# A decoder on one Trainium2 core: the C products of two of sixteen states in GpSimd's queue

## The reference, cut to what matters

```
xz = x @ Win;  xi, z = split(xz)
xi = silu(causal_dwconv(xi));  dt_in, B, C = split(xi @ Wx)      # 8, 16 and 16 columns
dt = softplus(dt_in @ Wdt + bdt);  A = -exp(Alog)
h[t, d, s] = exp(dt[t, d] * A[d, s]) * h[t-1, d, s] + dt[t, d] * xi[t, d] * B[t, s]
y[t, d]    = sum over s of h[t, d, s] * C[t, s]  +  xi[t, d] * D[d]
out = (y * silu(z)) @ Wout
```

## Time and profile before

| | us |
|---|---|
| median of three runs | 5442.49 |
| the profiled execution, its own time | 5428.83 |
| span of its trace | 5427.1 |
| the state-space stage in it | about 0 to 2475 |
| VectorE busy in 75 to 2475 | 2319 of 2400 |
| GpSimd busy in 75 to 2475 | 1974 of 2400 |
| TensorE's granted clock there, share of full speed | 0.91 |

### The profile page before, as it was taken

The page is one execution under the profiler, slowest core; times in us unless marked ns, Lnnn a source line. Parts: engine busy times, 40 slices in busy tenths (PEclk is TensorE's granted clock), DMA queues, the critical chain, the costliest instruction groups (busy, mean ns, idle before and its releaser), DMA issues. The chain is left out here.

```text
span 5427.1 us, 104523 instructions
## 1 busy us (share of the span) xinstructions
PE 4056.8 (75%) x29692; PEld 2331.6 (43%) x29692; DVE 4319.6 (80%) x8453; ACT 2781.0 (51%) x6469; POOL 3163.7 (58%) x3426
## 2 busy tenths in 40 slices
PE   5878778887787778874888678883747788688843
PEld 2333333333333333332666456652735666466611
DVE  5999999999999999994888767763356777666678
ACT  4555555555555555552777534434654445344434
POOL 5888888878888888874777533326452222333302
PEclk8998999889989989986999889995877888799955
DMA  2111111111110111102655366544125555465511
GB/s 84 67 49 54 69 68 68 42 62 69 68 69 33 69 68 68 69 37 46 105 102 102 60 119 110 104 88 151 57 89 107 95 96 95 82 112 102 98 39 31
DMA packets 320209, 420.99 MB, mean 78 GB/s; under 512 B 40000, under 2 KB 301712, under 8 KB 309136
## 3 DMA queue, kind: packets, MB, share of 16 engines
q1 hardware_dynamic: 315536, 408.35, 32.3%
q0 software_dynamic: 4352, 8.95, 0.5%
HBM read 307.65 MB, written 109.58 MB: 77 GB/s over the span
## 5 line engine op out<-in xcount | busy, mean ns | idle before, releaser
L2202 POOL TENSOR_TENSOR m_h<-m_dtu,m_Bb 128x512 f32<-128x512 f32 x1024 | 1598.1, 1590 | 148.4 <-PE bank L1835 146.1
L1835 PE MATMUL bank<-m_h,ident 128*128 128x512 f32 x2048 | 1245.2, 699 | 404.5 <-DVE m_h L2101 398.8
L1835 PEld LDWEIGHTS bank<-m_h,ident 128*128 128x128 f32 x2048 | 370.6, 210 | 1083.8 <-DVE m_h L2101 931.3
L2095 DVE TENSOR_TENSOR_SCAN m_h<-m_dA,m_h 128x512 f32<-128x512 f32 x512 | 771.0, 1506 | 0.5
L2101 DVE TENSOR_TENSOR m_h<-m_h,bank 128x512 f32<-128x512 f32 x1024 | 672.1, 656 | 14.4 <-PE bank L1828 14.4
L2095 DVE TENSOR_TENSOR_SCAN m_h<-bank,m_h 128x512 f32<-128x512 f32 x512 | 620.4, 1212 | 16.5 <-ACT bank L1983 9.5
L1983 ACT ACTIVATE bank<-m_dt,m_A 128x512 f32<-128x512 f32 x512 | 352.5, 688 | 378.6 <-DVE m_h L2095 273.6
L1983 ACT ACTIVATE m_dA<-m_dt,m_A 128x512 f32<-128x512 f32 x512 | 366.9, 717 | 350.1 <-DVE m_h L2095 343.4
L688 DVE TENSOR_REDUCE x_nm<-bank 128x4 f32<-128x308 f32 x512 | 242.7, 474 | 184.0 <-PE bank L359 181.1
L531 ACT ACTIVATE x_sm<-bank,x_nm 128x77 f32<-128x77 f32 x1024 | 318.2, 336 | 62.5 <-DVE x_nm L688 62.1
L688 DVE TENSOR_REDUCE f_nm<-bank 128x4 f32<-128x512 f32 x256 | 175.7, 687 | 120.2 <-PE bank L359 119.1
(11 more groups left out here) (425 smaller groups left out, 10366.2 us busy)
## 6 DMA issues: line engine op xcount, KB each, us to landing
m_Bb<-m_B SPq DMA_DIRECT2D x32, 4096.0 KB, 12.2
x_Ks<-x_k_parts SPq DMA_DIRECT2D x32, 462.0 KB
x_q_parts<-x_qp SPq DMA_DIRECT2D x32, 384.0 KB, 4.0
x_Qs<-x_q_parts SPq DMA_DIRECT2D x32, 384.0 KB
f_Ks<-f_k_parts SPq DMA_DIRECT2D x16, 768.0 KB
a_Ks<-a_k_parts SPq DMA_DIRECT2D x16, 768.0 KB
x_xp<-x_stage SPq DMA_DIRECT2D x32, 256.0 KB
x_Qs<-x_q_parts SPq DMA_DIRECT2D x32, 256.0 KB
```

What stands on the lines that cost most here:

```text
L1835: pe.matmul(banks[4 + c], ident[:], h[:, k % RING, :], start=(s == 0), stop=(s == NS - 1)).then_inc(s_ya.sem, 1)
L2095: v.tensor_tensor_scan(h[:, k % RING, :], decays[k % AHEAD], h[:, k % RING, :], 0.0, ALU.mult, ALU.add).then_inc(s_h.sem, 1)
L2202: pool.tensor_tensor(h[:, k % RING, :], dtu[:, d, c, :], Bb[:, d, s, :], ALU.mult).then_inc(s_dB.sem, 1)
```

## The change

The C products of the sixth and the twelfth state (index 5 and 11, that is steps 10, 11, 22 and 23 of each unit) go to POOL's queue, with their row of C read from SBUF. `Bb` gets two more rows for it, filled by the same broadcast DMA as B. Steps 10 and 11 are multiplied by POOL behind its input of step 14 and 15, steps 22 and 23 behind its input of step 26 and 27 (BEHIND = 4), and ahead of the side work listed for that step. TensorE adds them six steps behind instead of two, so the order of the adds changes, and the ring wait follows that order (`summed`). TensorE no longer spreads the two rows of C into PSUM. Ring, decay buffers and all side tables are unchanged.

```
+    ON_POOL = (5, 11)
+    ON_DVE = tuple(n for n in range(NS) if n not in ON_POOL)
+    BEHIND = 4
+    DSL, PSL = NC * len(ON_DVE), NC * len(ON_POOL)
...
+    def added_at(j):
+
+        late, k = j - LAG - BEHIND, j - LAG
+        return [n for n in (late,) if 0 <= n < SL and n // NC in ON_POOL] + [n for n in (k,) if 0 <= n < SL and n // NC in ON_DVE]
+
+    added = [k for j in range(SL + LAG) for k in added_at(j)]
...
+    def summed(n, k):
+
+        return (n, added.index(k) + 1) if k >= 0 else (n - 1, added.index(SL + k) + 1)
...
-        Bb = sb("Bb", [P, 2, NS, GT])
+        Bb = sb("Bb", [P, 2, NS + len(ON_POOL), GT])
...
-                sp.dma_start(Bd[d], xd[BROW:BROW + NS, :]).then_inc(s_Bd.sem, 16)
+                sp.dma_start(Bd[d, 0:NS], xd[BROW:BROW + NS, :]).then_inc(s_Bd.sem, 16)
+                for j, s in enumerate(ON_POOL):
+                    sp.dma_start(Bd[d, NS + j:NS + j + 1], xd[CROW + s:CROW + s + 1, :]).then_inc(s_Bd.sem, 16)
...
             def add(n, k):
...
-                pe.wait_ge(s_hC.sem, s_hC.at(n, k + 1))
+                if s in ON_POOL:
+                    pe.wait_ge(s_hP.sem, s_hP.at(*times_pool(n, k)))
+                else:
+                    pe.wait_ge(s_hC.sem, s_hC.at(*times(n, k)))
...
-                    if k >= LAG:
-                        add(n, k - LAG)
-                    elif begins:
+                    for state in added_at(k):
+                        add(n, state)
+                    if k < LAG and begins:
                         add(n - 1, SL - LAG + k)
-                    if k % 2 == 1 and k // 2 + 1 < NS:
+                    if k % 2 == 1 and k // 2 + 1 in ON_DVE:
                         spread_C(n, d, k // 2 + 1)
...
-                    if k:
+                    if k and (k - 1) // NC in ON_DVE:
                         times_C(v, n, k - 1)
...
-                pool.wait_ge(s_ya.sem, s_ya.at(n, k + 1 - RING))
+                pool.wait_ge(s_ya.sem, s_ya.at(*summed(n, k - RING)))
...
+            def times_C(n, d, k):
+                s = k // NC
+                pool.wait_ge(s_h.sem, s_h.at(n, k + 1))
+                pool.tensor_tensor(h[:, k % RING, :], h[:, k % RING, :], Bb[:, d, NS + ON_POOL.index(s), :], ALU.mult).then_inc(s_hP.sem, 1)
...
                     inputs(2 * g + d, g, d, k)
+                    if k >= BEHIND and (k - BEHIND) // NC in ON_POOL:
+                        times_C(2 * g + d, d, k - BEHIND)
                     for what in side(POOL_AT, g, d, k):
                         work(what, g, d)
```

More of the change, by code:

```diff
@@ L1593, in side, with times, times_pool @@
                 yield what
+    def added_at(j):
+        late, k = j - LAG - BEHIND, j - LAG
+        return [n for n in (late,) if 0 <= n < SL and n // NC in ON_POOL] + [n for n in (k,) if 0 <= n < SL and n // NC in ON_DVE]
+    added = [k for j in range(SL + LAG) for k in added_at(j)]
+    assert sorted(added) == list(range(SL)) and added[-NC:] == [SL - 2, SL - 1]
+    def summed(n, k):
+        return (n, added.index(k) + 1) if k >= 0 else (n - 1, added.index(SL + k) + 1)
+    def times(n, k):
+        c = k % NC
+        return n, NC * ON_DVE.index(k // NC) + c + 1
+    def times_pool(n, k):
+        c = k % NC
+        return n, NC * ON_POOL.index(k // NC) + c + 1
     with ExitStack() as st:
@@ L1600, in sem @@
             return Count(nc.alloc_semaphore(f"m_{name}"), per)
-        Bd = nc.dram_tensor("m_B", (2, NS, GT), F32, kind="Internal").ap()
+        Bd = nc.dram_tensor("m_B", (2, NS + len(ON_POOL), GT), F32, kind="Internal").ap()
         flip = sb("flip", [P, P])
@@ L1653, in mamba @@
         s_hi = sem("C_hi"); s_rest = sem("C_rest"); s_mid = sem("C_mid"); s_Cs = sem("C_lo"); s_Csh = sem("C_moved")
-        s_Bd = sem("B_stored", 16); s_Bb = [sem(f"B_spread{d}", 16) for d in range(2)]
+        s_Bd = sem("B_stored", 16 * (1 + len(ON_POOL))); s_Bb = [sem(f"B_spread{d}", 16) for d in range(2)]
         s_ab = sem("abs", 4); s_z = sem("exp_abs"); s_w1 = sem("one_plus"); s_ln = sem("log"); s_e = sem("correction")
         s_d1 = sem("log_corrected"); s_dr = sem("dt_raw"); s_dtu = sem("dtu"); s_dt = sem("dt")
-        s_C = sem("C_spread", NS); s_dA = sem("decay", SL); s_dB = sem("input", SL); s_h = sem("state", SL)
-        s_hC = sem("state_C", SL); s_ya = sem("summed", SL); s_yd = sem("y_D", 2); s_yz = sem("y_gated")
+        s_C = sem("C_spread", len(ON_DVE)); s_dA = sem("decay", SL); s_dB = sem("input", SL); s_h = sem("state", SL)
+        s_hC = sem("state_C", DSL); s_hP = sem("state_C_by_pool", PSL); s_ya = sem("summed", SL); s_yd = sem("y_D", 2); s_yz = sem("y_gated")
         s_var = [sem(f"var{n}") for n in range(3)]
@@ L1713, in spread_B @@
                 sp.wait_ge(s_dB.sem, s_dB.at(n - 1))
-                sp.dma_start(Bd[d], xd[BROW:BROW + NS, :]).then_inc(s_Bd.sem, 16)
+                sp.dma_start(Bd[d, 0:NS], xd[BROW:BROW + NS, :]).then_inc(s_Bd.sem, 16)
+                for j, s in enumerate(ON_POOL):
+                    sp.dma_start(Bd[d, NS + j:NS + j + 1], xd[CROW + s:CROW + s + 1, :]).then_inc(s_Bd.sem, 16)
                 sp.wait_ge(s_Bd.sem, s_Bd.at(n + 1))
                 sp.dma_start(Bb[:, d].rearrange("p s t -> p (s t)"),
-                             Bd[d].rearrange("s t -> (s t)").rearrange("(a n) -> a n", a=1).to_broadcast([P, NS * GT])).then_inc(s_Bb[d].sem, 16)
+                             Bd[d].rearrange("s t -> (s t)").rearrange("(a n) -> a n", a=1).to_broadcast([P, (NS + len(ON_POOL)) * GT])).then_inc(s_Bb[d].sem, 16)
             def store(g, l):
@@ L1826, in spread_C @@
                     pe.wait_ge(s_Csh.sem, s_Csh.at(n + 1))
-                pe.wait_ge(s_hC.sem, s_hC.at(n, 2 * s - 2))
-                pe.matmul(banks[2 + s % 2], selC[:, s, :], Cs[:, d, :], start=True, stop=True).then_inc(s_C.sem, 1)
+                at = ON_DVE.index(s)
+                pe.wait_ge(s_hC.sem, s_hC.at(n, NC * (at - 1)))
+                pe.matmul(banks[2 + at % 2], selC[:, s, :], Cs[:, d, :], start=True, stop=True).then_inc(s_C.sem, 1)
             def add(n, k):
@@ L2099, in times_C @@
                 v.wait_ge(s_h.sem, s_h.at(n, k + 1))
-                v.wait_ge(s_C.sem, s_C.at(n, s + 1))
-                v.tensor_tensor(h[:, k % RING, :], h[:, k % RING, :], banks[2 + s % 2], ALU.mult).then_inc(s_hC.sem, 1)
+                at = ON_DVE.index(s)
+                v.wait_ge(s_C.sem, s_C.at(n, at + 1))
+                v.tensor_tensor(h[:, k % RING, :], h[:, k % RING, :], banks[2 + at % 2], ALU.mult).then_inc(s_hC.sem, 1)
             def prologue(v, ch):
@@ L2130, in unit @@
                     scan(v, n, d, k)
-                    if k:
+                    if k and (k - 1) // NC in ON_DVE:
                         times_C(v, n, k - 1)
-                    elif not (isinstance(g, int) and n == 0):
+                    elif not k and not (isinstance(g, int) and n == 0):
                         times_C(v, n - 1, SL - 1)
```

## The result

The changed kernel takes 5516.77 us (median of 4 runs, 5513.89 to 5523.94), the kernel before 5444.12 beside it (5440.62 to 5452.83): ratio 1.0136, interval [1.012, 1.0153]. It is slower by 73 us; 26 were forecast, and the time lies above the range. The profiled execution has a span of 5512.2 us (before 5427.1) at a granted clock of 0.857 (before 0.865).

What follows compares the result with a forecast made beforehand. VectorE, 97% busy in the stage, looked like the only bound, with the SBUF way it shares with POOL some 89% full as a second. +1.7 us per pair of units gave 5442.5 + 26 = 5468 us, range 5420 to 5505.

Steps and rivals of the forecast that it cites:

- The pair: POOL operations and VectorE operations with two SBUF operands never overlap; a POOL product holds this shared way 1.14 us.
- Direction 1, steps 14 to 28: POOL's products delay dt and scans 27 and 28, so the unit takes 2.3 us more instead of 2.3 less.
- POOL's wait for the logarithm: POOL's idle time before dt in direction 1, 4.97 us in the unit read, would be gone or near zero.
- scans 27 and 28 wait: In direction 1 these two scans would idle behind POOL's inputs, 1 to 2 us each.
- Direction 0, dtu behind the late slot: Step 23's late add delays input 31 and dt; dtu idles about 2.8 us, unit 0.6 us less.
- so the products themselves are covered: In direction 0, steps 22 to 31, POOL is far ahead, with much of its 146.1 us of ring waits there.
- Odd scans' mean above 1505 ns: Sign in the changed trace: VectorE's odd scans would take longer in the mean than their 1505 ns before.
- POOL's wait before far: Sign in the changed trace: POOL, which idled 91.1 us before far, would no longer idle there.
- DMAs: Two more one-row DMAs and a broadcast of 18 rows for 16, 1.5 us more by size: no cost.
- Sum: A pair of units takes 2.3 - 0.6 = 1.7 us more; sixteen give +27, less the last unit +26.
- The outer bound of direction 0: At most 3.2 us more per direction-0 unit, with TensorE's 4.7 us growing by up to 3.8 at 1.2 GHz.

Runs made afterwards that it cites:

- e3: The kernel before, with POOL multiplying four more 128x512 tiles per unit into a tile that nothing reads: 5508.74 us, ratio 1.0135.
- e9: The changed kernel with states 6 and 10, adds four steps behind, and VectorE multiplying them from SBUF rows in direction 1: 5458.63 us, ratio 1.0047.
- e2: The kernel before, VectorE doing all products, with TensorE's adds of steps 10, 11, 22 and 23 six steps behind: 5520.46 us, ratio 1.0155.
- e7: The changed kernel with TensorE adding POOL's four steps four steps behind instead of six: 5470.83 us, ratio 1.0078.
- e1: The changed kernel with the C products of states 5 and 11 left out on both engines and adds in the old order: 5350.24 us, ratio 0.9836.
- e4: The changed kernel with POOL's C products cut to 8 of 512 columns, all waits kept: 5421.91 us, ratio 0.9972.
- e8: The changed kernel with states 6 and 10 and adds four steps behind instead of six: 5438.1 us, ratio 1.0016.
- e12: The changed kernel with states 6 and 10 on POOL in direction 0 only, adds four steps behind there, direction 1 as before: 5380.58 us, ratio 0.9883.
- e5: The changed kernel with POOL's product behind the side work of its step, so o_pow goes ahead of it: 5514.56 us, ratio 1.0155.
- e6: The changed kernel with states 5 and 10 on POOL instead of 5 and 11: 5500.81 us, ratio 1.0136.
- e11: The changed kernel with states 8 and 10 on POOL in direction 0 only, adds four steps behind there, direction 1 as before: 5379.67 us, ratio 0.9880.

## Why the prediction was right or wrong

**The pair.** Right as a mechanism. POOL's product took 1.26 us where it met nothing, and never less: 1854 ns in the mean, 235.4 us for 127. In e3 such operations alone cost direction 1 1.8 us; e9 shows the same hold on VectorE's own product.

**Direction 1, steps 14 to 28.** The size is right (+2.1 for +2.3), POOL's wait for the logarithm is gone (0.0 before L2211, where it was 74.6), and scans 27 and 28 wait as forecast (1.9 and 0.6 us for 1 to 2 each). But the working was too narrow. e2, without any product on POOL, also gives +2.1 there: the odd scans take 1.5 us more per unit and e 0.5, so late slots make POOL's operations meet them more often. By the single runs the products cost 1.8, the late adds 2.1 and the relief gives 0.9; I named one of the two costs and counted the relief as used up. That the sum came within 0.2 us is in part luck.

**Direction 0, dtu behind the late slot.** The mechanism was right: ring slot of step 23, input 31, dt, dtu, in each of the sixteen units; e2 shows it by itself and e7 takes it away. The size was 4.1 and not 2.8. TensorE's part, from the end of step 25's product to the end of the add of step 23, was put at 4.7 us and took 5.9 (1380.30 to 1386.22), because the clock was low. I had kept that for the bound, as something that happens in 3 of 16 units. But the change takes two steps' adds away just ahead of it, TensorE idles 3.20 us there, and the clock is low in all sixteen. That is 1.2 of the missing 1.3 us, an estimate from one unit's rows. POOL's lead was also gone by then (input 30 waits 2.10 us for its slot), but input 31 has to wait for the add of step 23 in any case.

**Direction 0, "so the products themselves are covered".** This is the step that failed, and with it the sum: +3.75 us for -0.6. I took POOL's 146.1 us of ring waits for slack in which anything could be put. But the products stand in POOL's queue ahead of o_pow, on which ScalarE's normalisation, tu, u and TensorE's z hang. Before, o_pow started 0.08 us after its operand and u without a wait. Over the runs u's wait follows o_pow's delay: at most 0.2 us where o_pow starts 0.08 us after its operand (e1, e2, e4, e8 to e12), 1.2 where it is 1.09 or 2.33 (e5, e3), 2.5 where it is 3.26 (the changed kernel, e6, e7). e8, which moves the products clear of o_pow, brings direction 0 from 81.1 to 78.7 us. It moves the late slots with them, and the scans' waits go too, so not all of the 2.4 us need be o_pow's.

From run to run direction 0 falls apart like this. The relief and the products together were forecast at -3.3 us and are -0.9 in e8; the products ahead of o_pow at nothing, and are 2.4 (e7 less e8); the late slot at 2.8, and is 2.3 (the change less e7). So nearly all of the miss is the products: they were neither covered nor harmless to what stands behind them. The late slot's wait is longer than forecast, but the unit gets only 2.3 of its 4.1 us back when it goes.

**Odd scans' mean above 1505 ns.** Wrong in sign: 1422. I had counted VectorE's loss as held time, where it came as waits: idle time grew by 145 us, while its busy time fell by 56 where the 124 products ahead of the last dtu alone are 124 * 0.57 = 71, so held time grew by 15. The sign fails as a sign: scans that waited for POOL aren't short (the 17 odd ones took 2.14 us in the mean, since POOL's next operation had begun), and the mean is low in e1 too (1451), which has no such waits. What lowers it is that fewer odd scans of direction 0 meet POOL: 60 of 255 took over 1.3 us, where 114 did. In e8 it is 1586.

**POOL's wait before far.** It fell from 91.1 to 22.6 us, and was forecast to go.

**DMAs.** Costed at nothing, and nothing was seen: the broadcast landed in 13.9 us, forecast 12.2 + 1.5, and no row waits for it.

**Sum.** Forecast 16 * (2.3 - 0.6) = +27; measured 16 * 3.75 + 15 * 2.11 = +92 by the mean units, 89 by the last dtu. The outer bound of direction 0 was +3.2, worked from a low clock at the unit's end. The clock was low there, but it cost some 1.2 us and not 3.8; what took direction 0 past the bound is u's wait.

## What to carry to other kernels

Idle time of an engine is not room for work: ask what stands behind the new operation in that engine's queue, and whether the engine's lead depends on it. Take the work off one engine where nothing short waits behind it (direction 0, clear of o_pow, adds as early as possible) and leave it where the two engines share the way to SBUF; that took 17.6 us (0.3%) off the stage here, with 1.2% off the medians, and the same work in both directions cost 1.4%. When work is put off, look at the engine that then has nothing to do: TensorE idled for 3.20 us and ran its next adds at the lower clock. Measure the gain as well as each cost by itself: e2 and e3 each look like the whole loss, and only with e1 do the parts come near the sum.

## What the runs showed of the hardware that I had not expected

VectorE's 128x512 product takes 0.66 us in the mean with an operand in PSUM, in every kernel here, and 0.66 to 1.70 us, 1.31 in the mean, with both in SBUF while POOL works (e9).

After 3.20 us in which TensorE had nothing to do, its matmuls ran at a granted clock of 0.57 for the next 4 us, and two adds took 3.79 us in place of about 1.8. An item of 16 partitions is held too: L2070 took 1637 ns in the mean in e8, 945 before.

The stages behind, with code unchanged, take different times in the profiled executions. From the last dtu to the end of the span (some 110 us of it are the end of the state-space stage): before 3024.7, after 3020.8, e3 3034.5, e1 3008.0, e8 3010.7, e9 to e12 2999.6 to 3003.6 us. The other runs lie between these. The clock of a stretch there (2600 to 4000) differs by 0.02 between kernels:

After:

```profile
2600.00:4000.00 1400.00, 1013.86 (x11525) 727.73 (x11526) 909.60 (x2422) 704.84 (x2918) 686.29 (x1173) 0.85 0.52 99
```

e11:

```profile
2600.00:4000.00 1400.00, 1060.38 (x11898) 790.26 (x11896) 907.38 (x2464) 750.72 (x2935) 687.73 (x1154) 0.87 0.49 97
```

The two stretches don't hold quite the same work, as the kernels reach them at different times, and the kernel before, which is not faster behind the stage, has 0.88 there. Over the whole of the stages behind, the mean clock lies between 0.832 and 0.837 in all kernels. Whether the state in which the stage behind starts explains the up to 35 us was not tried. It stays open, and so does that part of e1's, e11's and e12's gain.
